# A gated cross-attention and mixture-of-experts layer: another order for the last three token steps, and the shared first layer ahead of the softmax rows' transposes on TensorE

## The reference, cut to what matters

```python
# attention over 64 context tokens, 16 heads of 64
q = layernorm(x) @ Wq + bq;  k, v = ctx @ Wk + bk, ctx @ Wv + bv
x = x + tanh(g_xattn) * (softmax(q k^T / 8) v @ Wo + bo)
# feed-forward: a shared expert, and the best 2 of 8 experts for each token
h      = layernorm(x)
scores = sigmoid(h @ W_gate_router);  sel = top_k(scores + expert_bias, 2)
shared = (silu(h @ Wg_s) * (h @ Wu_s)) @ Wd_s
routed = sum over sel of weight * ((silu(h @ Wg[e]) * (h @ Wu[e])) @ Wd[e])
x = x + tanh(g_ffn) * (shared + routed)
```

## Time and profile before

| | us |
|---|---|
| median of 3 runs | 307.86 |
| lowest, highest | 304.25, 309.23 |
| the profiled execution | 305.99 |
| its span, first to last instruction | 304.2 |

### The profile page before, as it was taken

The page is one execution under the profiler, slowest core; times in us unless marked ns, Lnnn a source line. Parts: engine busy times, 40 slices in busy tenths (PEclk is TensorE's granted clock), DMA queues, the critical chain, the costliest instruction groups (busy, mean ns, idle before and its releaser), DMA issues.

```text
span 304.2 us, 6562 instructions
## 1 busy us (share of the span) xinstructions
PE 277.8 (91%) x1746; PEld 249.2 (82%) x1747; DVE 239.6 (79%) x691; ACT 159.8 (53%) x414; POOL 172.9 (57%) x234
## 2 busy tenths in 40 slices
PE   2899989999999899999996978988799999999994
PEld 1788768898897798999886966877699899999983
DVE  0489989999999789989989477379877776777694
ACT  1453475666766555573553243654355555556631
POOL 8012226787758876887855877638635344444440
PEclk9999999999999999999998699999999999999999
DMA  6999994133359999913121123322334343435797
GB/s 191 365 285 326 267 298 129 42 98 104 103 170 306 307 304 321 269 45 106 35 70 56 53 78 106 100 55 73 101 110 120 108 111 111 126 113 166 260 316 239
DMA packets 45007, 49.74 MB, mean 164 GB/s; under 512 B 3929, under 2 KB 41651, under 8 KB 44979
## 3 DMA queue, kind: packets, MB, share of 16 engines
q1 hardware_dynamic: 39938, 39.37, 45.0%
q0 software_dynamic: 3408, 8.46, 8.2%
q10 hardware_dynamic: 1632, 1.57, 1.5%
HBM read 21.67 MB, written 28.64 MB: 165 GB/s over the span
## 4 chain that ended last, share of the span: by engine, by line
PE 54%; DVE 26%; issue 7%; ACT 5%; POOL 3%; DMA 3%; SPq 1%; DVEq 0%; ACTq 0%; POOLq 0%
PE bank L1401 6%; PE bank L1403 5%; PE bank L1402 5%; PE scores_ps L1401 4%; PE scores_ps L1403 4%; PE scores_ps L1402 4%; DVE pT_lo L1129 4%; DVE probs L1152 4%; DVE row_sum L1136 3%; PE bank L1347 3%; DVE row_max L1146 3%; DMA Wk_sb<-in_L_xattn_Wk_dram 3%; PE bank L1598 2%; PE scores_ps L1438 2%; PE bank L1438 2%
## 5 line engine op out<-in xcount | busy, mean ns | idle before, releaser
L699 POOL DMA_INDIRECT routed_dram<-probs,sct_idx x39 | 38.4, 983 | 50.4 <-ACT probs L911 49.0
L649 POOL TENSOR_TENSOR probs<-probs,row_inv 128x1024 f32<-128x1024 f32 x16 | 30.5, 1909 | 25.8 <-DVE row_inv L1140 25.6
L1401 PE MATMUL bank<-AB_hi,pT_hi 128*128 128x256 f32 x128 | 38.1, 298 | 2.2 <-DVE pT_lo L1129 2.2
L613 POOL DMA_INDIRECT rows_dram<-xn,slot_i x32 | 32.0, 1001 | 12.5 <-issue 10.5
L1403 PE MATMUL bank<-AB_hi,pT_lo 128*128 128x256 f32 x128 | 36.8, 288 | 0.0
L1402 PE MATMUL bank<-AB_lo,pT_hi 128*128 128x256 f32 x128 | 36.8, 288 | 0.0
L768 ACT ACTIVATE probs<-probs 128x1024 f32<-128x1024 f32 x16 | 16.9, 1058 | 29.2 <-DVE probs L1152 29.2
L1401 PE MATMUL scores_ps<-AB_hi,xnT_hi 128*128 128x512 f32 x64 | 26.5, 414 | 1.9 <-DVE xnT_lo L1122 1.7
L1401 PEld LDWEIGHTS bank<-AB_hi,pT_hi 128*128 128x128 f32 x128 | 25.2, 197 | 2.7 <-issue 2.5
L1403 PE MATMUL scores_ps<-AB_hi,xnT_lo 128*128 128x512 f32 x64 | 25.3, 395 | 0.0
L1402 PE MATMUL scores_ps<-AB_lo,xnT_hi 128*128 128x512 f32 x64 | 25.3, 395 | 0.0
(11 more groups left out here) (248 smaller groups left out, 884.4 us busy)
## 6 DMA issues: line engine op xcount, KB each, us to landing
rows_dram<-pad_rows SPq DMA_DIRECT2D x10, 1040.0 KB, 15.8
rows_dram<-pad_rows SPq DMA_DIRECT2D x8, 780.0 KB, 12.6
AB_free<-routed_dram SPq DMA_DIRECT2D x8, 512.0 KB, 4.8
probs<-rows_dram SPq DMA_DIRECT2D x30, 130.0 KB, 2.1
raw_buf<-in_L_ffn_Wg_dram SPq DMA_DIRECT2D x8, 192.0 KB, 2.5
raw_buf<-in_L_ffn_Wu_dram SPq DMA_DIRECT2D x8, 192.0 KB, 2.9
out_dram<-x_sb ACTq DMA_DIRECT2D x6, 256.0 KB, 2.9
pT_hi<-rows_dram SPq DMA_DIRECT2D x9, 130.0 KB, 2.1
```

The source lines that it names most:

```text
L613: nc.gpsimd.indirect_dma_start(rows_dram[:, :], bass.IndirectOffsetOnAxis(ap=slot_i[:, t, k:k + 1], axis=0), xn2[:, t % KEEP, :], None).th ...
L649: nc.gpsimd.tensor_tensor(pr, pr, row_inv[:, :].unsqueeze(2).to_broadcast([P, H, KV]), ALU.mult).then_inc(norm_done, 1)
L699: nc.gpsimd.indirect_dma_start(routed_dram[:, :], bass.IndirectOffsetOnAxis(ap=sct_idx[(k - 2) % (2 * RING)][:, 0:1], axis=0), y_sb[ks][:, ...
L1401: nc.tensor.matmul(out_ap, a_hi, b_hi, start=first, stop=False)
```

## The change

All steps: on PE, `shared_up(t-2)` goes ahead of `transpose_p(t)`. On POOL, `norm_factors(3)` (step 5) goes ahead of the multiply of that step.

Step 13: `choose(3)`, `rank(3)` and `place(3)` leave this step. POOL puts tile 7 ahead of the multiply and tile 8 at the end (before: tile 7 and half of 8, both at the end).

Step 14: ACT does `high_p(14)` ahead of the exponentials of tile 15. DVE does `choose(3)` behind `hidden(12)` and `place(3)` at the end. PE does `rank(3)` at the end, behind `transpose_xn2(13)`. POOL puts nothing.

Step 15: PE does `late_transpose` and `late_down` of tiles 0 and 1 between `transpose_p(15)` and `attention(15)`, into the scores' banks, free by then; ACT has `late_hidden(0)`, `late_hidden(1)` behind `high_p(15)` and the two `late_copy` at the end. POOL puts tile 9 alone (before: 10 and 11).

Behind the loop: the down projections begin at tile 2, and POOL puts tiles 10 to 15 (twelve DMAs; before: 12 to 15, eight).

```diff
+        EARLY = 2
+        early_ps = [scores_ps[:, 512 * z:512 * z + 512] for z in range(EARLY)]
-        lhT_ps = [pT_ps[z % 2] if z < NB else bank[2 + (z - NB) % 2] for z in range(T)]
+        lhT_ps = [early_ps[z] if z < EARLY else pT_ps[z % 2] if z < NB else bank[2 + (z - NB) % 2] for z in range(T)]
 # POOL, step
+                if t == 5:
+                    norm_factors(3)
-                if 6 <= t < T - 3:
+                if 6 <= t < T - 2:
                     put_tile(t - 6)
-                if t == T - 2:
-                    put_tile(8, [1])
                 if t == T - 1:
-                    put_tile(10)
-                    put_tile(11)
+                    put_tile(9)
...
-                if t == 5:
-                    norm_factors(3)
...
                 if t == T - 3:
-                    put_tile(7)
-                    put_tile(8, [0])
-                if t == T - 2:
-                    put_tile(9)
+                    put_tile(8)
             token_loop(step, between, first=-3)
             second_norm(T - 1)
-            for t in range(BATCHES[4][0], T):
+            for t in range(10, T):
                 put_tile(t)
 # ACT, step
-                if t == 1:
+                if t == T - 2:
+                    high_p(t)
+                    exponentials(m)
+                elif t == 1:
...
-                high_p(t)
+                if t != T - 2:
+                    high_p(t)
+                if t == T - 1:
+                    late_hidden(0)
+                    late_hidden(1)
...
+                if t == T - 1:
+                    late_copy(0)
+                    late_copy(1)
 # DVE, step
-                if t == T - 3:
-                    choose(3)
                 if inside(v) and v not in BY_POOL:
                     hidden(v)
+                if t == T - 2:
+                    choose(3)
...
-                    if t == (z + 1 if b == 3 else z + 2) and b >= MOVED:
-                        place(b)
...
                 if t >= T - 2:
                     low_xn2(w, 1 - q)
+                if t == T - 2:
+                    place(3)
 # PE, step
-                transpose_p(t)
                 if inside(v):
                     shared_up(v, q)
+                transpose_p(t)
...
+                if t == T - 1:
+                    pe.wait_ge(sub_done, T)
+                    late_transpose(0)
+                    late_transpose(1)
+                    late_down(0)
+                    late_down(1)
...
                     attention(t)
-                if t == T - 3:
-                    rank(3)
                 if t >= T - 2:
                     transpose_xn2(w)
+                if t == T - 2:
+                    rank(3)
```

More of the change, by code:

```diff
@@ L215, in flamingo_layer @@
         cmp_ps = route[:, 160:160 + Q * E].rearrange("p (j e) -> p j e", e=E)
-        lhT_ps = [pT_ps[z % 2] if z < NB else bank[2 + (z - NB) % 2] for z in range(T)]
+        EARLY = 2
+        early_ps = [scores_ps[:, 512 * z:512 * z + 512] for z in range(EARLY)]
+        lhT_ps = [early_ps[z] if z < EARLY else pT_ps[z % 2] if z < NB else bank[2 + (z - NB) % 2] for z in range(T)]
         sum_ps = [bank[4], scores_ps[:, 0:512], scores_ps[:, 512:1024], bank[5]]
-        late_ps = [[att_ps, scores_ps[:, 0:512], scores_ps[:, 512:1024]][z % 3] if z < NB else sum_ps[z - NB] for z in range(T)]
+        late_ps = [early_ps[z][:, D:2 * D] if z < EARLY else
+                   ([att_ps, scores_ps[:, 0:512], scores_ps[:, 512:1024]][z % 3] if z < NB else sum_ps[z - NB])[:, 0:D]
+                   for z in range(T)]
         diag = [late_hid[:, n, 0:P] for n in range(2 * (T - NB))]
@@ L863, in _ @@
             token_loop(step)
-            def late_copy(z):
-                act.wait_ge(late_done, z + 1)
-                nc.scalar.activation(late_out[:, z, :], late_ps[z][:, 0:D], ACT.Copy).then_inc(late_read, 1)
             gates_of_shared(T - 2)
             second_norm(T - 1)
-            late_hidden(0)
+            late_hidden(2)
             high_xn2(T - 1, (T - 1) % 2)
-            late_hidden(1)
-            late_copy(0)
+            late_hidden(3)
+            late_copy(2)
             gates_of_shared(T - 1)
-            for z in range(2, NB):
+            for z in range(4, NB):
                 late_hidden(z)
@@ L925, in _ @@
                 act.wait_ge(tail_summed, z - NB + 1)
-                nc.scalar.activation(x_sb[:, z, :], late_ps[z][:, 0:D], ACT.Copy).then_inc(tail_copied, 1)
+                nc.scalar.activation(x_sb[:, z, :], late_ps[z], ACT.Copy).then_inc(tail_copied, 1)
                 if z % 2:
@@ L1435, in late_down @@
                 pe.wait_ge(lhT_done, z + 1)
-                after(pe, late_read, min(z, NB) - 2)
+                after(pe, late_read, 2 if z == 2 else min(z, NB) - 2)
                 for k in range(2):
-                    mm = nc.tensor.matmul(late_ps[z][:, 0:D], lhT[z % 2][:, k, :], Wds[:, k, :], start=(k == 0), stop=(k == 1 and z < NB))
+                    mm = nc.tensor.matmul(late_ps[z], lhT[z % 2][:, k, :], Wds[:, k, :], start=(k == 0), stop=(k == 1 and z < NB))
                 mm.then_inc(late_done, 1)
             def tail_sum(z, weights, rows, last=False):
-                mm = nc.tensor.matmul(late_ps[z][:, 0:D], weights, rows, start=False, stop=last)
+                mm = nc.tensor.matmul(late_ps[z], weights, rows, start=False, stop=last)
                 if last:
@@ L1556, in _ @@
             pe.wait_ge(pT_lo_done, 2 * T)
-            late_transpose(0)
-            late_transpose(1)
+            late_transpose(2)
+            late_transpose(3)
             transpose_xn2(T - 1)
             pe.wait_ge(x2_done, T)
-            late_down(0)
+            late_down(2)
             rank(5)
             shared_up(T - 1, (T - 1) % 2)
-            late_transpose(2)
-            late_down(1)
-            late_transpose(3)
+            late_transpose(4)
+            late_down(3)
+            late_transpose(5)
             rank(6)
@@ L1569, in _ @@
             count(range(*BATCHES[6]), count_ps_done)
-            late_down(2)
-            for z in range(4, NB):
+            late_down(4)
+            for z in range(6, NB):
                 late_transpose(z)
```

3 lines of the change are left out of this document (added).

## The result

The changed kernel takes 312.82 us (median of 4 runs, 312.54 to 315.71); in the same comparison the kernel before takes 307.25 (4 runs, 304.25 to 309.23). The ratio is 1.0224, with a 95% interval of 1.0157 to 1.029: slower, by about 2%. That it is slower is shown; that it is so by more than 2% isn't, as the interval holds 1.02. The profiled execution took 312.84 with a span of 311.1; the earlier trace rows belong to one of 305.99 with a span of 304.2. The difference to explain is 6.85 us.

The account below looks back on a forecast made before the run. PE, busy 91% of the span, was taken as the bound, with the puts behind the loop hidden by only 1.7 us. 3.3 + 2.2 + 2.1 = 7.6 us on 305.99 gave 313.6 us, range 307 to 318.5.

Parts of the forecast that it names:

- the three terms of the sum: Later start of the experts 3.3 us, clock fall in steps 14 and 15 2.2, clock fall ahead of the experts 2.1.
- the prediction's own last line: It called itself wrong if PE isn't idle ahead of the experts, or if rank(3) doesn't wait.
- Steps 7, 14 and 15: Step 7 gains 0.9 us; step 14 pauses 1.1 us ahead of attention(14), then 3.3 in all; attention(15) ends 1.8 later.
- second_norm(15) ... 179.7: POOL behind the loop: tile 15's mean and variance are ready at 179.7, before 179.04.
- the last starts at 195.6: POOL behind the loop: the last of twelve puts starts at 195.6, before 189.74, at a pitch of 1.28 us.
- the first expert matmul ... comes at 202.7: Start of the experts: the gather sets it, 3.3 us later than 199.38, with PE's own way (196.7) hidden behind.
- The first fall of the clock, 2.2: Step 14's pauses bring half clock from about 169.5 to 176.4, costing 2.2 us, between 0 and 4.5.
- The first rival: The clock stays up, once or twice: 311.4, 311.5 or, without both falls, 309.3 us; chance 0.32.
- The second fall, 2.1: PE idle some 4.5 us ahead of the experts, then half clock over their first 5 us: 2.1 us, between 0 and 3.5.
- the 3.3: Start of the experts: tile 15, twelve puts, then the gather come late, so the first expert matmul is 3.3 us later.
- The third rival: Puts stay hidden, PE sets the experts' start, 1.3 us sooner: 304.7 us, 302.4 if choose(3) costs nothing; chance 0.14.

Follow-up runs that it names:

- e1_puts: Changed kernel with the puts of tiles 10 and 11 back in step 15, behind tile 9: 308.76 us, ratio 1.008 to the kernel before.
- x6_before_again: The kernel before, unedited, profiled a second time: 306.35 us.
- x1_gap: Changed kernel with one pause in POOL's row of puts, until the rows of tile 12 have landed: 313.51 us, ratio 1.026 to the kernel before.
- x7_puts_as_before: Changed kernel with all puts back where the kernel before has them: 308.68 us, ratio 1.009 to the kernel before.
- x2_before_row: Kernel before with only the puts of tiles 10 and 11 moved behind the loop, twelve in a row: 312.26 us, ratio 1.0223.
- x3: Changed kernel with 32 memsets added at the start of VectorE's list: 313.83 us, ratio 1.0232 to the kernel before.
- x5: Changed kernel with seventeen small chained VectorE operations ahead of its wait for PE's count: 313.69 us, ratio 1.0258 to the kernel before.
- e4_order: Kernel before with only shared_up ahead of transpose_p and norm_factors(3) ahead of step 5's multiply: 306.25 us, ratio 0.999.
- x9_puts_no_late: Changed kernel with all puts back as in the kernel before and no late block in step 15: 306.83 us, ratio 1.0036 to the kernel before.
- after: The changed kernel itself, all parts of the change in: 312.82 us, ratio 1.0224 to the kernel before.
- e2_choose13: Changed kernel with choose(3), rank(3) and place(3) back in step 13: 312.50 us, ratio 1.0232 to the kernel before.
- e3_no_late: Changed kernel without the late block in step 15, its work back behind the loop: 314.41 us, ratio 1.0274 to the kernel before.
- x4_puts_choose: Changed kernel with tiles 10 and 11 put in step 15 and choose(3), rank(3), place(3) in step 13: 309.71 us, ratio 1.0121 to the kernel before.

## Why the prediction was right, and where it was not

The time (312.8 for 313.6) and the sign came out, the place too: the loss is in the start of the experts, and the puts behind the loop make it. But of the three terms of the sum the first was there without setting anything, and two were not there; something unforeseen filled their place. By the prediction's own last line ("I am wrong if PE isn't idle ahead of the experts") its mechanism was wrong: PE went from its last down projection to the transposes of the gathered tile at 204.64 without an idle time.

*Steps 7, 14 and 15*: right, to a few tenths. Pauses of 1.07, 2.08 and 0.70 for forecast 1.1, 2.2 and 1.1; `attention(15)` ends 0.5 later than before, for 1.8 less the 0.9 of step 7.

*"second_norm(15) ... 179.7", "the last starts at 195.6"*, both less 0.9: 178.8 and 194.7 forecast, 178.59 and 196.47 measured. POOL's start and pitch were right (1.27 for 1.28). The last put is 1.8 later since its row numbers came late, out of the stand. I had treated the row of puts as something that costs POOL's time alone.

*"the first expert matmul ... comes at 202.7"*: 206.04. This step failed. It has the gather as the last to arrive (199.0, measured 200.68) and PE "hidden behind it", forecast through its list by 196.7. PE was through at 204.64. So the wait that ended last was PE's own list, held up by waits of ACT beside the row of puts. PE's account: the chain of waits has 1.44 us of "issue" and 3.92 of "another core or an unknown queue" at the stand, 5.4 in all; then, from 195.31 to 204.64, PE does in 9.3 us six down projections and four pairs of transposes, which at the pitches of the earlier trace rows are 6 x 0.86 + 4 x 0.22 = 6.0, so half clock costs 3.3; the two tiles done in step 15 give 2.2 back, and `attention(15)` takes 0.5. Together 7.0, of the 6.7 seen.

*The first fall of the clock, 2.2*: not there; the windows above have 1.00 there. The first rival said so with 0.32. It isn't a rule either way: e1_puts has the same pauses 1.2 us earlier (1.07, 2.04 and 0.70), and there the clock falls (windows as above):

```profile
165.00:166.00 1.00, 0.00 (x0) 1.00 0.00 0
166.00:167.00 1.00, 0.18 (x2) 1.00 0.00 0
167.00:168.00 1.00, 0.43 (x4) 0.87 0.03 8
168.00:169.00 1.00, 0.86 (x3) 0.50 0.00 0
```

The same pauses gave both outcomes, and in the kernel before so did one and the same pause of 2.24 us (the earlier trace rows and x6_before_again). The Trainium skill ("TensorE: Matmul & The Clock Gate", Part 1) tells of a monitor that runs freely and doesn't start anew with the kernel, and explains by it why the clock of one kernel rises at another point from run to run. These traces agree with that, and don't prove it.

*The second fall, 2.1*: there was one, but 10 us earlier and behind another pause, not behind an idle PE ahead of the experts. Where PE did wait there, for 1.51 us in x1_gap, it came. By the experts' start the clock was whole again, and the term behind it is 105.06 - 104.82 = 0.2.

So that 3.3 + 2.2 + 2.1 = 7.6 met 6.85 was luck for the most part. The chain of the 3.3 was there, with the tile at 202.8, but hidden behind PE; the 6.66 came from the stand and the half clock behind it. Which of it would be left without the stand no run of the full row shows. e1_puts and x7_puts_as_before, where PE does wait for the gather, show that the chain can set the start. The third rival (the puts stay hidden, PE sets the start of the experts) came half true in a form I had not thought of: PE does set it, and later.

*By parts*, from the ratios: taking back the puts of tiles 10 and 11 returns 1.4% (1.0224 - 1.008), the late block is put at 0.5%, all else at 0.4% (1.0036, at most 0.7% by its interval). The parts don't simply add: the same four puts cost 2.2% by themselves in the kernel before (x2_before_row). The place of `choose(3)` and the new order of the first layer can't be told from nothing.

*Open*: why waits of DVE and ACT end late beside a row of puts, and PE's don't. It isn't fetching of DVE's instructions (x3), and DVE's arithmetic goes on (x5). The DMA engines are far from full (shares of 0.36 and 0.42 at 192 to 194). Whether it is the number of puts, their 128 rows each or the increments with which each of them reports was not tried. Nor is there one length from which it begins: with six puts issued, `hot_val` came 0.04 us behind PE's count in the profile of before, 0.5 in x6_before_again, 1.4 in e4_order (187.55 for 186.11) and 2.0 in x9_puts_no_late.

## What to carry to other kernels

A row of indirect DMAs on GpSimd can cost more than its pitch: four puts fewer in the row behind the loop were worth 1.4 to 2.2% here, while a pause put into the full row was worth nothing. Look for waits of VectorE and ScalarE that fall beside such a row, and keep them ahead of it or the row short. Work pulled forward can stand ahead of what feeds the longest chain, as the late block did; look first at what the last step's result releases. A forecast time that is met says nothing of its mechanism: compare the signs. When a wait in the trace ends on "remote" though its producer is long done, look at what another engine was doing without a break at that time, and test it by making that one row in the kernel before.

## What the runs showed of the hardware

Beside ten unbroken puts of 0.96 us at a pitch of 1.27, waits of DVE and ACT on results of PE ended up to 7.0 us behind those results (after: 194.55 for 187.73; e2_choose13: 194.11 for 187.11). DVE's ended 2.3 to 3.0 us behind the start of the last put of the row: 2.3 in e3_no_late (190.00) and x4_puts_choose (177.05), 2.8 in after (191.79), 2.9 in x2_before_row (189.08) and x3_pad (192.72), 3.0 in e2_choose13 (191.15); ACT's in e3_no_late 3.7. DVE's waits on its own semaphore were late there too, by 0.28 to 0.54 us, and only late in the row (x5_busy). PE's waits on ACT in the same stretches ended 0.05 and 0.06 us behind ACT's copies (after 190.78, x5_busy 194.38). And one pause of PE, 2.24 us ahead of `attention(14)`, brought the clock to half in one execution of the kernel before and left it at 1.00 in another.
